# Softmax maxima of a cross-attention: one strided reduction, or running elementwise maxima between the evacuations

## What is computed

```python
q = rmsnorm(heads(layernorm(x) @ Wq.T), q_norm_w)     # 8 batches, 32 heads, 64 queries, 128
k = rmsnorm(heads(ctx @ Wk.T), k_norm_w)              # 8 batches, 8 heads, 1601 keys, 128
v = heads(ctx @ Wv.T)
scores = einsum('bhqd,bhkd->bhqk', q, k) / sqrt(128) + mask
attn = softmax(scores)                                # the maximum is taken over the 1601 keys
x = x + (attn @ v) @ Wo.T
```

## Time and profile before

| | |
|---|---|
| median of 3 runs | 2884.36 us (2882.27 to 2886.12) |
| the profiled execution's own time | 2894.39 us |
| its span | 2892.7 us |
| busy TensorE, VectorE, ScalarE, GpSimd | 2543.8, 2068.6, 1265.3, 1457.4 us |
| line 536, the strided reduction | 64 instructions, 376.9 us |
| TensorE's granted clock over the span | 0.956 of full speed |

### The profile page before, as it was taken

The page is one execution under the profiler, slowest core; times in us unless marked ns, Lnnn a source line. Parts: engine busy times, 40 slices in busy tenths (PEclk is TensorE's granted clock), DMA queues, the critical chain, the costliest instruction groups (busy, mean ns, idle before and its releaser), DMA issues. The chain is left out here.

```text
span 2892.7 us, 49172 instructions
## 1 busy us (share of the span) xinstructions
PE 2543.8 (88%) x18636; PEld 1800.3 (62%) x18636; DVE 2068.6 (72%) x2779; ACT 1265.3 (44%) x1816; POOL 1457.4 (50%) x895
## 2 busy tenths in 40 slices
PE   7879989998998999899899989989996988999985
PEld 3457767776776777677677767766774444444443
DVE  6857676776777677766766777677767558888884
ACT  4544444353434444444434444453443435455441
POOL 0136666665766576656755666566654002232221
PEclk9989999998999999999999999999998989999997
DMA  6420010001001000100010010000000811112100
GB/s 202 129 88 10 8 54 9 8 9 54 14 10 54 9 8 9 54 9 14 8 56 9 8 54 9 8 11 10 5 5 27 267 52 52 51 64 89 51 15 23
DMA packets 89193, 117.48 MB, mean 41 GB/s; under 512 B 6942, under 2 KB 58910, under 8 KB 88990
## 3 DMA queue, kind: packets, MB, share of 16 engines
q1 hardware_dynamic: 86718, 107.09, 11.0%
q0 software_dynamic: 2272, 7.50, 1.0%
HBM read 96.74 MB, written 17.83 MB: 40 GB/s over the span
## 5 line engine op out<-in xcount | busy, mean ns | idle before, releaser
L636 POOL TENSOR_TENSOR rk<-z,half 128x13 f32<-128x13 f32 x64 | 156.0, 2438 | 695.9 <-DVE z L516 695.9
L242 PE MATMUL pF<-w_h,ctx_h 128*128 128x256 f16 (+1 forms) x1664 | 460.9, 277 | 0.0
L242 PE MATMUL pF<-w_l,ctx_h 128*128 128x256 f16 (+1 forms) x1664 | 459.1, 276 | 0.0
L242 PE MATMUL pF<-w_h,ctx_l 128*128 128x256 f16 (+1 forms) x1664 | 458.2, 275 | 0.0
L173 POOL TENSOR_TENSOR p_l<-S,p_h 128x1792 f16<-128x1792 f32 x126 | 430.7, 3444 | 0.0
L536 DVE TENSOR_REDUCE mx<-S 128x256 f32<-128x3328 f32 x64 | 376.9, 5889 | 2.2
L526 DVE SCALAR_TENSOR_TENSOR S<-pS,rk,mask 128x256 f32<-128x256 f32 x832 | 347.1, 475 | 15.6 <-PE pS L242 7.4
L402 ACT ACTIVATE k_h<-pF 128x400 f16<-128x400 f32 (+1 forms) x256 | 129.1, 504 | 510.4 <-PE pF L242 510.4
L242 PE MATMUL pF<-ctx_h,w_h 128*128 128x400 f16 (+1 forms) x1024 | 348.0, 340 | 4.0 <-PEq L759 4.0
L242 PE MATMUL pF<-ctx_l,w_h 128*128 128x400 f16 (+1 forms) x1024 | 347.6, 339 | 0.0
L242 PE MATMUL pF<-ctx_h,w_l 128*128 128x400 f16 (+1 forms) x1024 | 346.6, 338 | 0.0
(11 more groups left out here) (240 smaller groups left out, 5817.9 us busy)
## 6 DMA issues: line engine op xcount, KB each, us to landing
ctx_f<-ctxT_dram SPq DMA_DIRECT2D x24, 800.0 KB, 6.3
s_wst<-winG_dram SPq DMA_DIRECT2D x8, 1536.0 KB, 10.5
q_wst<-wqT_dram SPq DMA_DIRECT2D x8, 1024.0 KB, 7.1
o_scratch<-o_st SPq DMA_DIRECT2D x32, 256.0 KB, 2.6
p_ost<-o_scratch SPq DMA_DIRECT2D x16, 512.0 KB, 6.9
p_wst<-woT_dram SPq DMA_DIRECT2D x16, 512.0 KB, 7.7
s_wst<-winG_dram SPq DMA_DIRECT2D x8, 1024.0 KB, 7.2
m_wost<-woutG_dram SPq DMA_DIRECT2D x8, 1024.0 KB, 5.4
```

The costliest lines, as they stand in the source:

```text
L242: mm = pe.matmul(out, x, y, start=first and j == 0, stop=final and j == 2)
L636: pool.tensor_tensor(rk[:, s % 2, 0:KT], z[:, s % 2, 0:KT], half[:, 0:KT], ALU.pow).then_inc(rk_ok, 1)
```

## The change

The reduction on line 536 goes. In its place stand seven elementwise maxima in each unit, `running_maximum` for p = 1 to 6 and one last `maximum`. The tile `mx` of 256 columns becomes `mx2`, twice as wide: it holds the running maxima of the even and of the odd tiles. The last instruction folds one half onto the other. Each waits for the evacuation just ahead of it and for the running maximum before it, and the semaphore `mx_ok` now counts seven in a unit. `keys(3)` moves ahead of the last two.

```diff
@@
-        mx = sb("mx", [P, QC], F32)
+        mx2 = sb("mx2", [P, 2, QC], F32)
@@
             def turn_maxima(b, s):
 
                 u = U * b + s
-                wait(pe, mx_ok, u + 1)
+                wait(pe, mx_ok, 7 * (u + 1))
                 wait(pe, o_ok, 2 * (u - 1))
                 for h in range(2):
-                    mm = pe.transpose(pO[s % 2][:, 1, h * P:(h + 1) * P], mx[:, h * P:(h + 1) * P], ident[:, :])
+                    mm = pe.transpose(pO[s % 2][:, 1, h * P:(h + 1) * P], mx2[:, 0, h * P:(h + 1) * P], ident[:, :])
                 mm.then_inc(mt_ok, 1)
@@
+            def running_maximum(b, s, p):
+
+                u = U * b + s
+                wait(dve, s_out, 7 * u + p + 1)
+                if p == 1:
+                    dve.tensor_tensor(mx2[:, :, :], S[:, s % 2, 0:2, :], S[:, s % 2, 2:4, :], ALU.max).then_inc(mx_ok, 1)
+                elif p < 6:
+                    wait(dve, mx_ok, 7 * u + p - 1)
+                    dve.tensor_tensor(mx2[:, :, :], mx2[:, :, :], S[:, s % 2, 2 * p:2 * p + 2, :], ALU.max).then_inc(mx_ok, 1)
+                else:
+                    wait(dve, mx_ok, 7 * u + 5)
+                    dve.tensor_tensor(mx2[:, 0, :], mx2[:, 0, :], S[:, s % 2, KT - 1, :], ALU.max).then_inc(mx_ok, 1)
+
             def maximum(b, s):
-                u = U * b + s
-                wait(dve, s_out, 7 * (u + 1))
-                dve.tensor_reduce(mx[:, :], S[:, s % 2, :, :].rearrange("p t q -> p q t"), AX.X, ALU.max).then_inc(mx_ok, 1)
+                wait(dve, mx_ok, 7 * (U * b + s) + 6)
+                dve.tensor_tensor(mx2[:, 0, :], mx2[:, 0, :], mx2[:, 1, :], ALU.max).then_inc(mx_ok, 1)
@@
                     evacuate(b, s, 1)
                     evacuate(b, s, 2)
+                    running_maximum(b, s, 1)
                     keys(1)
+                    running_maximum(b, s, 2)
                     evacuate(b, s, 3)
                     evacuate(b, s, 4)
+                    running_maximum(b, s, 3)
                     keys(2)
+                    running_maximum(b, s, 4)
                     evacuate(b, s, 5)
                     evacuate(b, s, 6)
+                    running_maximum(b, s, 5)
+                    keys(3)
+                    running_maximum(b, s, 6)
                     maximum(b, s)
-                    keys(3)
                     overall(b, s)
```

## The result

| | before | after |
|---|---|---|
| median, us | 2883.71 (4 runs, 2882.27 to 2886.12) | 2901.53 (4 runs, 2896.90 to 2903.54) |
| ratio | 1 | 1.0059, 95% interval 1.0041 to 1.0076 |
| span of the profiled execution, us | 2892.7 | 2898.2 |
| granted clock over the span | 0.956 | 0.965 |

The changed kernel is 18 us slower; 56 had been forecast.

The account below looks back on a forecast made before the run. The prediction took TensorE, through its waits and granted clock, to bound the kernel. +39 us at full speed and +17 us for the clock made +56, giving 2940 us on the median, with an eight-in-ten range of 2868 to 2985.

Parts of the forecast that it names:

- What bounds the kernel: TensorE, busy 1867 of 2070 us in the stage, sets the pace; only its waits and its clock move the time.
- The signs named for being right: Trace signs: line 304 hardly waiting, waits for `S` over 150 us, longer maxima, longer L181 and L183, `squares` awaiting `sq_l`.
- DVE and POOL exclude each other, at 0.14 us less than the full wait: When both read two SBUF tensors, the second waits for the first's end, less 0.14 us of its own start.
- the rival of free passage: At line 304's wait: maxima run beside POOL unhindered, 1.5 us of each 1.82 us wait goes; 2745 us, chance 7%.
- Unit after an even one: Maxima waiting for POOL delay the score matmuls 3.2 us; net +1.4 us in each of 25 units.
- after an odd one: Score matmuls come 2.0 us late and POOL's last squares hold TensorE; net +0.55 us in each of 32 units.
- the heavy rival: Nothing is hidden: POOL loses the full 4.3 us a unit and bounds it, +2.4 us on 57 units; 3035 us, 8%.
- Units with `ctx_split`: In 7 units DVE is the bound; it gives up 5.8 us and takes on 3.9 us: -2 us each.
- Sum at full speed: Unit terms together: 35 us after even units, 18 after odd ones, less 14 for `ctx_split` units: +39 us.
- The clock: Stalls move from the transposes to score matmuls; 12 more falls to half speed at 1.4 us each: +17 us.
- the second kind: Units after an odd one, 32 of them; their stall was to stay near 2 us, their falls unchanged.
- The profiled execution: The profiled run took 2894.4 us, 10 above the median; the forecast gave 2950 us on it, 2940 on the median.

Follow-up runs that it names:

- experiment 1: Both kernels with POOL's low halves of the probabilities and its sums left out: changed kernel 2735.3 us, kernel before 2849.2 us.
- a_busy: Changed kernel with extra matmuls ahead of the score matmuls that stall, 22 in units with odd s, 12 in the others: 2897.4 us, ratio 1.0039.
- b_busy: Kernel before with 12 extra matmuls (1.3 us) ahead of the transposes of line 304: 2851.5 us, ratio 0.9890.
- experiment 2: Extra matmuls put into TensorE's stalls in both kernels: kernel before 2851.5 us, changed kernel 2897.4 us.
- experiment 3: Kernel before with 12 extra matmuls between the transposes of line 304 and the squares, the stall left in place: 2935.9 us (a single run).
- b_nopool: Kernel before with POOL's low halves of the probabilities and its sums over the tiles left out: 2849.2 us, ratio 0.9881.
- tail: Changed kernel with all five wide maxima moved behind the last evacuation, ahead of the last key piece: 3017.6 us, ratio 1.0465.

## Why the prediction was right in direction and wrong in size

- *What bounds the kernel.* Right. The waits of TensorE and its clock moved the time.
- *The signs named for being right.* All came: line 304 hardly waits, the wait for `S` is over 150 us, the new maxima average well over 0.69 us with a longest of 3.1 us (line 538), L181 and L183 grew (medians 3.76 and 2.14 us), and `squares` waits for `sq_l`.
- *DVE and POOL exclude each other, at 0.14 us less than the full wait.* Right. The first maximum ended 0.55 us behind L181, as a 0.69 us instruction 0.14 ahead would; L183 lost 0.32 of the 0.33 us reckoned, and leaving POOL's instructions out turned +18 into -114 us (experiment 1). So the rival of free passage describes what happens without POOL's long instructions, not this kernel.
- *Unit after an even one, +1.4, after an odd one, +0.55.* Measured +1.2 and +0.8. Over 24 and 24 ordinary units the two errors nearly cancel. Two slips in the working changed nothing of this: 5 x 0.60 and 2 x 0.34 us of issue spacing are 3.7, not 3.9, and in the heavy rival 1035.0 lies 2.7 us behind 1032.3, not 2.4.
- *Units with `ctx_split`, -2 us each.* They went from some 41.2 us to 37.4. Time at half speed in these seven fell from 75 to 48 us, which is 1.9 us of work in each; the full-speed part is near -2.
- *Sum at full speed, +39.* Nearly right: 46 us between a_busy and b_busy, some 17 of which are a_busy's own, leave 29 (experiment 2); the two profiles give 5.5 us between the spans and 29 us less lost at half speed, so 34.
- *The clock, +17 us.* This is the step that failed, and it failed in sign. I took it that "in the second kind it stays near 2 us, so I leave its falls as they are" and "in the first it becomes 3.2 us, and I expect a fall every time". The stall did stay near 2 us, at 1.8. But the falls behind it went, 1 of 33, and at 3.0 us only 13 of 23 had one. I had read a fall as a matter of how long TensorE idles. The runs show that the length alone does not decide: at the transposes, where 26 matmuls of 128 columns follow (the squares), twelve dense ones put ahead of the squares took the falls away, and where in time a stall ends counts too (experiment 3). Which of the two spared the stalls at s5 is open. In the two profiles time at half speed in the units fell from 154 to 96 us, 29 us of work at full speed: the term was about -29 there, not +17. Half of it, 14 us, fell in the seven `ctx_split` units, whose falls the forecast had left as they are. By the medians the term is smaller, about -11 to -14 (35 us of falls before, 21 to 24 after, experiment 2), and with it 29 us at full speed come to +15 to +18, against +18 measured.
- *The profiled execution.* That of before took 10 us more than its median, that of after 2 us less than its own. Ten runs of the kernel before on one chip spread from 2876.9 to 2895.1 us, four of b_busy, with the falls largely out, from 2851.0 to 2853.2. The granted clock of each run goes with it: 0.964 in the fastest of the ten and 0.956 in the slowest, 0.972 to 0.974 in b_busy. So falls that differ from run to run make most of this spread.

Left open: why the end of a stall at some positions brings a fall and at others not, why in b_nopool only half of those at the bad positions do, and whether the move to s5 would spare the clock at other positions.

## What to carry to other kernels

Before splitting one long VectorE reduction, whose only tensor input is strided, into elementwise steps with two SBUF inputs, look at what GpSimd runs beside them: each step that meets one of its instructions on two SBUF tensors waits for the end of it, and what stands behind the step on VectorE waits too. Price a wait of TensorE by where it stands as well as by its length, for here a stall of 1.8 us with narrow matmuls behind it cost the clock in 27 of 63 cases, and with dense ones close behind in 1 of 63. A forecast of falls from a few stalls of one trace is uncertain by more than this change was worth. And where the bound engine waits for a long operation elsewhere, first look for independent work in its own queue that can be moved into the wait: one moved line gained 69 us here, half of it clock, where 448 short instructions in the place of 64 long ones lost 18.

## What the runs showed of the hardware that I had not expected

- The granted clock fell behind 27 of 63 stalls of 1.8 us followed by transposes and 128-column matmuls, behind 1 of 63 with twelve 256-column ones between the two, and behind 1 of 33 in the midst of scores and values, 28 of which ended at positions where the first kind had 1 fall in 37.
- With light work behind it, the same stall of 1.8 us had a fall in 26 of 26 cases or in 1 of 37, by where in time it ended (experiment 3).
- Exclusion with POOL's shortest instructions was not cheap. In tail, where I had expected POOL in instructions of 0.7 to 0.95 us (the trace has the squares' low halves, 0.95 us alone, beside the maxima), the four maxima of line 541 still took 1.14 us in the mean:

```profile
L541 DVE TENSOR_TENSOR mx<-mx,S 128x512 f32<-128x512 f32 x256 | 291.2, 1138 | 28.8 <-DVE mx L538 2.8
```
